# Cross-attention and a 4-bit-grid FFN on one core: weights rounded in the first batches and kept in DRAM, the split of q and k on other engines, the last rows' outputs in banks of their own, the first FFN rows' operations in another order

## The reference

```python
# x (8, 512, 256), ctx (8, 512, 256), bias (1, 512, 512), mask (8, 512); 16 heads of 16
x = x + xattn(layernorm(x), ctx, ctx, bias, mask, in_proj_w, in_proj_b, out_proj_w, out_proj_b)
x = x + ffn(layernorm(x), w_gate (704, 256), w_up (704, 256), w_down (256, 704))

def xattn(query, key, value, ...):
    q, k, v = projections, per head
    scores = einsum('bthd,bshd->bhts', q * 0.25, k) + attn_bias; masked keys get the lowest float
    return softmax(scores) @ v, all heads side by side, @ out_proj_w.T + out_proj_b

def ffn(x, w_gate, w_up, w_down):        # fp4_linear rounds both of its operands
    h = silu(fp4_linear(x, w_gate)) * fp4_linear(x, w_up)
    return fp4_linear(h, w_down)         # rounding: blocks of 16, scale = max/6, values to the grid 0, .5, 1, 1.5, 2, 3, 4, 6
```

## Time and profile before

| | |
|---|---|
| time, median of 3 runs | 916.71 us (916.69 to 917.88) |
| the profiled execution's own time | 915.36 us |
| its span, first to last instruction | 913.1 us |
| PE / DVE / ACT / POOL busy | 880.4 / 724.0 / 606.4 / 536.3 us |
| granted TensorE clock | full throughout |

### The profile page before, as it was taken

How to read it: one execution, slowest core, us unless ns; L and a number is a source line. 1 busy time by engine, 2 the same in 40 slices (tenths; PEclk the granted TensorE clock), 3 DMA queues, 4 the chain that set the end, 5 groups by cost and what they waited for, 6 DMA issues and landing times.

```text
span 913.1 us, 20279 instructions
## 1 busy us (share of the span) xinstructions
PE 880.4 (96%) x6797; PEld 705.0 (77%) x6797; DVE 724.0 (79%) x1913; ACT 606.4 (66%) x1093; POOL 536.3 (59%) x504
## 2 busy tenths in 40 slices
PE   8989999999999999999999999999979999999997
PEld 7767777777777777778777777777668888888885
DVE  7867677767767767867776679899779999999994
ACT  5777777767777777777777777787745555555542
POOL 4987867867776786777778556886312222232221
PEclk9999999999999999999999999999999999999999
DMA  6685434333342433445243342610000000000000
GB/s 192 192 250 153 129 74 126 101 88 114 90 133 72 118 105 74 116 103 133 61 116 108 70 136 74 173 39 1 2 0 13 19 17 23 17 17 18 18 18 29
DMA packets 50413, 76.12 MB, mean 83 GB/s; under 512 B 5072, under 2 KB 21840, under 8 KB 50320
## 3 DMA queue, kind: packets, MB, share of 16 engines
q1 hardware_dynamic: 50192, 74.80, 30.1%
q10 hardware_dynamic: 128, 0.13, 0.1%
HBM read 45.16 MB, written 29.36 MB: 82 GB/s over the span
## 4 chain that ended last, share of the span: by engine, by line
PE 81%; ACT 6%; issue 5%; DVE 4%; DMA 2%; SPq 1%; POOL 0%; ACTq 0%; DVEq 0%
PE psum L1371 27%; PE psum L1518 12%; PE psum L1472 11%; PE psum L1768 9%; PE psum L1758 4%; PE psum L1760 4%; PE psum L1759 4%; PE psum L1433 3%; PE psum L1393 3%; ACT att L811 2%; PE psum L1399 1%; PE psum L1410 1%; ACT att L818 1%; DVE att L1183 1%; ACT att L762 1%
## 5 line engine op out<-in xcount | busy, mean ns | idle before, releaser
L1183 DVE CUSTOM_DVE_ANT_0 att<-psum,att 128x512 f32<-128x512 f32 x512 | 341.7, 687 | 144.6 <-PE psum L1472 142.8
L654 POOL TENSOR_TENSOR att<-att,neg_max 128x512 f32<-128x512 f32 x312 | 326.2, 1056 | 158.0 <-DVE neg_max L1183 155.4
L1371 PE MATMUL psum<-ident,att 128*128 128x128 f32 x2640 | 389.0, 274 | 18.0 <-ACT att L811 7.4
L1371 PEld LDWEIGHTS psum<-ident,att 128*128 128x128 f32 x2640 | 317.4, 140 | 86.0 <-ACT att L811 29.0
L811 ACT ACTIVATE att<-psum 128x512 f32<-128x512 f32 x512 | 297.9, 598 | 115.4 <-PE psum L1371 111.0
L1472 PE MATMUL psum<-stack 128*128 128x512 f32 x512 | 248.7, 487 | 3.5 <-DVE neg_max L1183 2.4
L736 POOL TENSOR_TENSOR att<-att 128x704 f32<-128x704 f32 x31 | 59.8, 1929 | 155.1 <-DVE att L1258 155.1
L818 ACT ACTIVATE att<-att,neg_max 128x512 f32<-128x512 f32 x200 | 144.2, 721 | 3.5 <-DVE neg_max L1183 3.4
L1472 PEld LDWEIGHTS psum<-stack 128*128 128x128 f32 x512 | 96.7, 189 | 36.7 <-issue 25.3
L1518 PE MATMUL psum<-att 128*32 128x256 f32 x2048 | 123.6, 382 | 0.0
L1518 PEld LDWEIGHTS psum<-att 128*32 128x32 f32 x2048 | 60.1, 109 | 44.0 <-issue 8.7
(11 more groups left out here) (125 smaller groups left out, 1057.2 us busy)
## 6 DMA issues: line engine op xcount, KB each, us to landing
stack<-qk_planes SPq DMA_DIRECT2D x124, 192.0 KB, 3.9
qk_planes<-q_hl SPq DMA_DIRECT2D x48, 256.0 KB
qk_planes<-k_hl SPq DMA_DIRECT2D x48, 256.0 KB
att<-in_fside_1xSxS_dram SPq DMA_DIRECT2D x32, 256.0 KB, 2.7
att<-in_ctx_dram SPq DMA_DIRECT2D x8, 512.0 KB, 7.5
out_dram<-att SPq DMA_DIRECT2D x32, 128.0 KB, 1.7
x<-in_x_dram SPq DMA_DIRECT2D x1, 2560.0 KB, 13.5
x<-in_x_dram SPq DMA_DIRECT2D x3, 512.0 KB, 6.1
```

Source lines behind the costliest of these rows:

```text
L654: pool.tensor_tensor(prob[:, slot, :], prob[:, slot, :], neg_max[:, slot:slot + 1].to_broadcast([P, S]), ALU.subtract).then_inc(less_pool, 1)
L1183: dve.tensor_tensor_reduce(out=prob[:, slot, :], in0=ps_score[:, SCORE_BANK[2 * S_ + r], :], in1=bias_m[:, tt, :], scale=-1.0, scalar=BIG, ...
L1371: return pe.transpose(out_, in_, ident[:, :])
```

## The change

Four things change.

1. **The split of q and k.** ACT writes the rounded high part from the bank itself, and DVE makes the low part from the same bank (bank + bias - high). POOL has no part in it, and the float32 buffers are gone. The scale is put into the transposed q weights. A bank is now free when DVE has made the low part: PE waits for `q_low`, `k_low`. (The second octet of batch 0 keeps a buffer, `second`.) DVE's work on q stands after step 12 and 28's second tile instead of in steps 13 and 29.
2. **The weights.** The nine pieces are rounded two per batch in batches 1 to 4 and one in batch 5, all in one buffer (`w_piece`, with `w_abs`). ACT issues the DMA that loads a piece (10 steps after the one before it began) and the one that stores the rounded piece in DRAM (7 steps after its begin). In batches 6 and 7 SP loads the rounded pieces from there into `w_slot`, and PE's transposes wait for these loads. `by_act` no longer gives ACT extra tiles in octets 13 and 14.
3. **The tail.** The down products of rows 29 and 30 go to banks 2 and 3 and wait for no output; that of row 31 waits for the outputs of rows 0 to 28.
4. **The head.** On DVE the rounding of row 0's h moves ahead, between the two halves of `take_out` of the last batch, both `out_stats` come after step 2, and in steps 2 and 3 `x_low` comes right after the product h.

```diff
-            return r == 1 and (s % 4 != 0 or n in (N_OCT - 3, N_OCT - 2))
+            return r == 1 and s % 4 != 0
-        WEIGHT_BEGIN = [(B - 2, 16), (B - 2, 20), (B - 2, 24), (B - 1, 1), (B - 1, 4), (B - 1, 7), (B - 1, 11), (B - 1, 14), (B - 1, 18)]
+        WEIGHT_BEGIN = [(1 + z // 2, 2 + 16 * (z % 2)) for z in range(PIECES)]
+        STORE, LOAD = 7, 10
+        def y_bank(m, par):
+            if is_row(m, ROWS - 3):
+                return psum[:, 2, 0:E]
+            return psum[:, 3, 0:E] if is_row(m, ROWS - 2) else ps_y[:, par, :]
...
 SP, weights_in
+                    sp.wait_ge(g_stored, 16 * (z + 1))
                     if z >= 6:
                         sp.wait_ge(gwT_ready, z - 5)
+                    sp.dma_start(w_slot[:, z % 6, :], rounded[z]).then_inc(gT_in[z % 6], 16)
...
 POOL
-            def low_q(m):
-                pool.wait_ge(q_high, m + 1)
-                pool.tensor_tensor(ql, q32, qh.bitcast(F32), ALU.subtract).then_inc(q_low, 1)
...
 ACT
-                act.activation(q32, src, ACT.Identity, bias=b_q4[:, o:o + 1], scale=SCALE).then_inc(q_taken, 1)
+                wait(act, q_plane, 48 * m)
+                act.activation(qh, src, ACT.Identity, bias=b_q4[:, o:o + 1]).then_inc(q_high, 1)
...
                 act.wait_ge(gw_mul, z + 1)
-                wait(act, gw_y, z if z < 3 else z - 1)
-                act.activation(wt(z), wq(z), ACT.Abs, scale=PULL).then_inc(gw_abs, 1)
+                wait(act, gw_y, z)
+                act.activation(w_abs, w_piece, ACT.Abs, scale=PULL).then_inc(gw_abs, 1)
+            def weights_store(z):
+                act.wait_ge(gw_q, z + 1)
+                act.dma_start(rounded[z], w_piece).then_inc(g_stored, 16)
+            def weights_load(z):
+                g, m = piece_rows(z)
+                dst = w_piece.rearrange("p (c n) -> p c n", c=2)
+                wait(act, g_stored, 16 * z)
+                ...
...
                 for z in pieces_at(b, S_, 3):
                     weights_abs(z)
+                for z in pieces_at(b, S_, STORE):
+                    weights_store(z)
+                for z in pieces_at(b, S_, LOAD):
+                    if z + 1 < PIECES:
+                        weights_load(z + 1)
...
 DVE
-                dve.wait_ge(q_taken, m + 1)
+                dve.wait_ge(q_high, m + 1)
                 wait(dve, q_plane, 48 * m)
-                dve.tensor_copy(qh, q32).then_inc(q_high, 1)
+                dve.scalar_tensor_tensor(ql, bank, b_q4[:, o:o + 1], qh.bitcast(F32), ALU.add, ALU.subtract).then_inc(q_low, 1)
...
-                    if S_ == 13 and not last:
-                        high_q(2 * b + 2)
                     if S_ == 17 and not last:
-                        high_k(2 * b + 2)
+                        low_k(2 * b + 2, 0, M1)
-                    if S_ == 29 and not last:
-                        high_q(2 * b + 3)
                     less_scores(b, S_, 1)
+                    if S_ in (12, 28) and not last:
+                        low_q(2 * b + 2 + S_ // 28, S_ // 28, M0)
...
             ffn_head(step, 1)
+            take_out(B - 1, 0, M0)
+            round_h_up(0, 0)
+            round_h_down(0)
+            take_out(B - 1, 1, M1)
+            ffn_head(step, 2)
             for i in range(2):
-                take_out(B - 1, i, (M0, M1)[i])
                 out_stats(B - 1, i)
-            ffn_loop(dve, step, 2)
+            ffn_loop(dve, step, 3)
...
 PE
-                        pe.wait_ge(q_taken, 2 * b + 3)
+                        pe.wait_ge(q_low, 2 * b + 3)
                     make_ot(4 * b - 1, M1 if last else M0)
...
-                    wait(pe, fout_ready, n - 3)
+                    if is_row(n - 3, ROWS - 1):
+                        pe.wait_ge(fout_ready, ROWS - 3)
+                    elif not (is_row(n - 3, ROWS - 3) or is_row(n - 3, ROWS - 2)):
+                        wait(pe, fout_ready, n - 3)
```

More of the change, by code:

```diff
@@ L198, in piece_rows, with two_loads @@
             return (q * 2) // IC, (q * 2) % IC
+        def two_loads(z):
+            g, m = piece_rows(z)
+            return g < 2 and m == IC - 2
         def loads_of(z):
-            return sum(32 if p[0] < 2 and p[1] == IC - 2 else 16 for p in map(piece_rows, range(z % 6, z + 1, 6)))
+            return sum(32 if two_loads(i) else 16 for i in range(z + 1))
         def lows_of(z):
@@ L545, in body @@
                 planes_k(2 * b + 1)
-                if last:
-                    sp.wait_ge(k_low, N_OCT)
-                    weights_in(range(5, 6))
                 stack_octet(2 * b + 1)
@@ L574, in body @@
                         sp.wait_ge(q_ready, N_OCT)
[L575 to L576 removed]
+                        weights_in(range(4, 6))
                     bias_again(b, 3)
@@ L692, in body @@
                             less_max(n, s, r)
-                    if S_ == 5 and first:
-                        low_q(1)
-                    if S_ == (6 if first else 1):
-                        low_k(2 * b + 1)
                     if S_ in (1, 3) and not first:
@@ L704, in body @@
                         rstd_of(b + 2)
-                    if S_ == 13 and not last:
-                        low_q(2 * b + 2)
-                    if S_ == 17 and not last:
-                        low_k(2 * b + 2)
                     if S_ in ((24, 26) if first else (19, 21)) and has_next2(b):
@@ L983, in ffn_step @@
                     x_high(n + 1, 1 - par)
-                m = n - 1
-                if live(m):
-                    act.wait_ge(fhy_ready, m + 1)
-                    wait(act, fhd_ready, m)
-                    act.activation(f_ha, f_hy[:, 1 - par, :], ACT.Abs, scale=PULL).then_inc(fha_ready, 1)
+                if live(n - 1) and not is_row(n, 1):
+                    h_abs(n - 1, 1 - par)
             batches(act, body)
@@ L1286, in step @@
                     dve.tensor_tensor(f_h, f_sil[:, 1 - par, :], ps_gu[:, I:2 * I], ALU.mult).then_inc(fh_ready, 1)
+                early = isinstance(n, int) and n < 4
+                if early and n >= 2:
+                    x_low(n, par)
                 if live(mx):
@@ L1324, in step @@
                     add_out()
-                if live(m2) and not tail:
-                    round_h_up()
+                if live(m2) and not tail and not is_row(m2, 0):
+                    round_h_up(m2, par)
                 if live(mx):
@@ L1332, in step @@
                                       ALU.mult).then_inc(fxy_ready, 1)
-                if live(m2) and not tail:
-                    round_h_down()
+                if live(m2) and not tail and not is_row(m2, 0):
+                    round_h_down(m2)
                 if live(mh) and not tail:
```

177 lines of the change are left out of this document (97 added, 80 removed).

## The result

The changed kernel takes 911.57 us (median of 5 runs, 911.48 to 912.5), the one before in the same session 916.76 us (5 runs, 916.69 to 917.88): a ratio of 0.9942, 95% interval 0.993 to 0.9954. The profiled execution took 911.48 us, its span 909.7 us; against the 913.1 us of before the span is 3.4 us shorter. The forecast gave 0.40 to a kernel faster by over 0.2%; it was faster by 0.58%.

What follows compares the result with a forecast made beforehand. PE was taken to set the time nearly everywhere, so changes count by PE's waits. 3.6 + 4.1 + 0.5 - 3.2 - 2.5 - 2.8 - 0.2 = -0.5 us on 916.71 gave 916.2 us, range 912.0 to 920.0.

Steps and rivals of the forecast that it cites:

- part 5: Batch 7: six rounding pieces leave DVE, six abs leave ACT, transposes and copies stay; -2.5 us, bounds 1.5 and 4.
- Part 1: Split of q and k: in step 12 of six batches PE waits for DVE's low part; 0.6 us each, +3.6 us.
- Part 2: Rounding in batches 1 to 5: PE waits 0.5 us at five first pieces, 0.4 at four second ones; +4.1 us.
- Part 3: DMA issues on ACT's queue: nine stores and eleven loads, nearly hidden, 0.025 us each; +0.5 us.
- Part 4: Batch 6: becomes like batch 5, since all its excess belongs to pieces that are gone; -3.2 us.
- Part 6: Tail: with own banks, products of rows 29 and 30 no longer wait for outputs of earlier rows; -2.8 us.
- Part 7: Head: `x_low(2)` ready 1.1 us earlier, but DVE's work up to `x_low(4)` is the same sum; -0.2 us.
- B: Rival: rounding is cheap, its product shorter where POOL has less to do, costing 1.3 us; 913.4 us, chance 0.34.
- C: Rival: DMA issues on ACT's queue only partly hidden, twenty cost 6 us in place of 0.5; 921.7 us, chance 0.16.
- D: Rival: cuts not all there, batch 7 gives 1.5 instead of 2.5, last row half of 2.8; 918.6 us, chance 0.12.

Runs made afterwards that it cites:

- before_noround: The kernel before with its rounding of weights left out; loads, stores, transposes and copies stay: 910.08 us, ratio 0.9919 to the kernel before.
- byact_old: The changed kernel with the old `by_act`, ACT again having eight more tiles in octets 13 and 14: 913.32 us, ratio 0.9951 to the kernel before.
- before_byact: The kernel before with only the edit of `by_act` made: 921.2 us, ratio 1.004 to the kernel before.
- after_noround: The changed kernel with the rounding's seven operations per weight piece left out, DMAs kept: 908.3 us, ratio 0.9894 to the kernel before.
- abs_late: The changed kernel with ACT's abs of a weight piece put behind the step's second exp: 910.29 us, ratio 0.9928 to the kernel before.
- early_q: The changed kernel with ACT's q copy at the ends of steps 11 and 27, DVE's low part after the second tile there: 902.82 us, ratio 0.9849.
- tail_old: The changed kernel with the old banks and waits of the last rows: 914.46 us, ratio 0.9975 to the kernel before.
- head_old: The changed kernel with the old order in the first rows (DVE, ACT's abs of row 0, POOL's work): 911.59 us, ratio 0.9939.
- control: The kernel before, unchanged, as a run of its own: 916.96 us, ratio 0.9996.

## Why the forecast was wrong, step by step

The step that failed is **part 5**: it let 2.5 us of batch 7 go, and 4.5 came back. That is 2.0 of the 4.6 us that were missed; the way from the span to the median, near the end of this list, hid another 1.8.

- **Part 5, batch 7, -2.5 us (bounds 1.5 and 4): the term that was mis-sized; 4.5 us.** Shown by four runs: the rounding took 3.3 us of batch 7 (`before_noround`), where 2.5 was let go on the ground that the copies of the transposes stay and bind. They stay, and did not bind those 3.3. The other 1.2 us is `by_act` (`byact_old`), an edit for which the sum had no term at all; there the copies did bind, each together with a tile that the edit took from ACT. Read singly in the old kernel it would have been priced with the wrong sign, at +4.6 us (`before_byact`).
- **Part 1, +3.6.** 0.6 us in each of batches 1 to 6 by `after_noround`, 3.5 in all, and it stands in steps 8 to 15 (21.40 us in place of 20.84). PE waits 1.38 us, forecast 1.3 to 1.4. Mechanism and size right.
- **Part 2, +4.1.** 3.8 by `after_noround`. Both places are where they were put: 0.40 us in steps 0 to 7 (forecast 0.5), 0.45 in steps 16 to 23 (forecast 0.4). `abs_late` shows that the first is ACT's and the second DVE's, as the part had it. ACT's wait before the abs was twice the forecast: ACT had been idle for 0.42 us before the exp of 345.40 already, which the 0.4 left out, and the product took 1.37 us. PE's wait was not longer.
- **Part 3, +0.5.** Nothing, by the equal batches of `after_noround`. The issues took 0.33 to 0.45 us, the two that come second of a pair 0.52 and 0.56. The row that the part rested on was a single issue; 1.5 us earlier in the same trace stand two in a row, which were not hidden:

```profile
18.60 1.43 ACTq L422 DMA_DIRECT2D stack<-q_hl  x2
20.08 0.69 ACT L767 ACTIVATE att<-psum,b_qk 128x512 f32<-128x512 f32 x1 [1.11 <-issue]
```

That the pairs of the changed kernel cost nothing is luck: they lay under the copy of q, and stuck out in `early_q`, where that copy has moved a step ahead.

- **Part 4, -3.2.** 3.3 by `before_noround`; batch 6 is 79.4 us, forecast 79.5.
- **Part 6, -2.8.** 2.8 (`tail_old`); row 30's products begin right behind row 29's, and from row 4's products to row 31's it is 211.94 us in place of 214.68, 2.74 less, where the part had 2.82 (904.75 in place of 907.57).
- **Part 7, -0.2.** Nothing (`head_old`). The wait of 2.2 us moved from row 2 to row 3, and row 4 is where it was, as the part said of it.
- **The sum.** Measured on the spans: 3.5 + 3.8 - 3.3 - 4.5 - 2.8 = -3.3, and -3.4 was seen. The forecast -0.5 differs by 2.9, of which 2.0 is part 5 and 0.8 parts 2 and 3; the rest is 0.1 us or 0.2 here and there.
- **From the span to the median.** The forecast added the change to a median that was 1.35 us above the profiled execution, without asking what the 1.35 us were. They are the clock of the section before. Over the 48 timed runs of the kernel before in the three sessions, by the granted clock averaged over the run, 14 with 1.00 have a median of 915.5 us, 9 with 0.998 one of 916.7, and 25 with 0.996 one of 918.3. The changed kernel has three runs with 1.00 (911.5 us), two with 0.998 (912.0 and 912.5) and none with 0.996. Like with like, the change is worth 4.0 us; the 5.2 us between the medians are 3.4 of span, 0.5 that went from what lies around the span (2.3 to 1.8 us; `before_byact` has it too, so it needs none of the parts priced here), and 1.3 of the old kernel's clock. That the wait gone from the tail is why the second drop no longer comes is likely: 0.996 was seen in 35 of the 85 runs of kernels with the old tail and in none of the 45 with the new one. The one pair that differs in the tail alone is thinner, 2 of 11 runs of `tail_old` and none of 5 of the changed kernel.
- **The rivals.** *B* came nearest by its total (913.4) and fell by its mechanism: with POOL at 55 to 56 us per batch the product did not get shorter but took the same 1.37 us in all nine places. In each, POOL's subtraction of a maximum ran beside it (348.60 to 349.64 beside 348.81 to 350.18). The Trainium skill, "GPSIMD Engine Reference", section "Key points", says that POOL contends with DVE instructions of two SBUF inputs; the trace agrees, with 18 of 18 products that ended 0.55 us after POOL's running instruction. But the prediction's reading of it, 0.76 us beside an idle POOL and 1.2 beside a busy one, does not hold: POOL was at work beside both products of 0.76 us, with 0.22 us of its instruction left. What counts is when in POOL's instruction the product begins, not how busy POOL is on average. *C* fell in the changed kernel, and its mechanism was seen at two places of `early_q`: 0.8 us in batch 3 and 0.2 in batch 4, each behind two issues in a row. *D* had the sign of part 5's error the wrong way round.

## What to carry to other kernels

A stage whose work is to be removed should be priced by what a batch without that work takes, not by what would still be left in it to bind: here the undisturbed batch gave batch 6 to 0.1 us, and batch 7, which has no undisturbed twin and was priced by an argument, was 2 us off. Every edit of the diff needs a term, the smallest line too, and it must be read in the kernel that it will stand in: moving four tiles per batch to POOL cost 4.6 us beside the rounding and gave 1.2 us without it. And when an operation on the other engine frees a bank, put it where it starts as soon as the bank is written, at the end of the step before: that was worth 8.8 us for q, more than the change as a whole gave. Whether the kernel before, whose wait there was 0.59 us, would gain by the same move was not tried.

## What the hardware showed that was not expected

- TensorE's granted clock fell to the 1.2 GHz level for 3.4 us after waits of PE of 2.2 and 1.5 us in some executions and not in others of the same kernel, and cost 1.2 and 1.5 us in `control`; the medians by the run's mean clock (915.5, 916.7 and 918.3 us at 1.00, 0.998 and 0.996) say the same. What decides it stays open.
- The twenty DMA issues on ACT's queue took 0.33 to 0.56 us in the changed kernel and were hidden. Two in a row were not hidden at three places: 1.43 us for both held ACT for 1.11 us in the kernel before, 0.52 us for the second held it for 0.34 us in batch 4 of `early_q`, and 1.32 us, beside an issue of SP, for 0.66 us in batch 3.
- DVE's product of two SBUF tiles of 128x512 and POOL's instructions took turns, a whole instruction at a time: 18 products of 0.76 to 1.56 us all ended 545 to 550 ns after the POOL instruction that was running when they began. In the changed kernel each began 0.2 us after a subtraction of 1.04 us, the costly side of it; placing it just ahead of the subtraction was not tried.
